# A denser routing product, a new order in the token blocks and a longer tile pipeline in a mixture-of-experts kernel

## The chip, the cores and the metric

One core of one Trainium2 chip runs the kernel. The metric is the device time of one execution in microseconds, lower is better. TensorE is called PE, VectorE DVE, ScalarE ACT, GpSimd POOL and SyncE SP. All of them run their own queue of instructions in order and meet at semaphores.

## The reference

```python
def reference(...):                       # x is (2, 2048, 256) f32
    x = x + attention(layernorm(x))       # 16 heads, causal; the change does not touch it
    xf = layernorm(x).reshape(-1, 256)    # 4096 tokens
    for j in range(2):
        residual = xf
        gate = xf @ router_W[j] + router_b[j]                  # 6 experts
        _, ids = top_k(gate + gate_bias[j], 2)
        sel = (ids[:, :, None] == arange(6)).any(axis=1)
        weights = softmax(where(sel, gate, -inf))
        h = einsum('nh,ehi->eni', xf, exp_Wup) + exp_bup[:, None, :]
        h = silu(einsum('eni,eij->enj', h, exp_Wg) + exp_bg[:, None, :]) * h
        eo = einsum('eni,eih->enh', h, exp_Wdown) + exp_bdown[:, None, :]
        s = (xf @ share_Wup + share_bup).reshape(-1, 2, 256)   # the shared expert
        s = silu(s @ share_Wg + share_bg) * s
        share_out = (s @ share_Wdown + share_bdown).sum(axis=1)
        y = residual + einsum('ne,enh->nh', weights, eo) + share_out
        xf = y * rsqrt(mean(y * y) + 1e-6) * norm_w[j]
    return x + xf.reshape(x.shape)
```

## The kernel before

`build_attention` comes first and leaves its result in DRAM (y_latent). `build_tokens`, the mixture, does the rest, and every edit is in it. It has two rounds c, one for each pass of the reference's loop. A round has eight blocks r of 512 tokens (blocks 0 to 7, then 8 to 15) and then 69 tiles t of 128 rows. A number in float32 is split into a high and a low part in the type fp32r (`_hi` by ACT, `_lo` by DVE or POOL as a difference), and a product is the sum of high x high, high x low and low x high.

A block of tokens. `turn(r)` turns the normalized tokens on PE into PSUM banks 6 and 7, `xt_hi` and `xt_lo` copy them to `xt`. `route(r)` (L1631) multiplies them with the router's weights; `choose(r)` (from L2258 to L2279) ranks six experts per token on DVE, `tanh` on ACT and `weigh` on DVE make the two weights. `shared_up(r, k)` for k = 0 to 3 (L1666) makes two products of 6 matmuls each with 512 columns; `silu(r, k)` (L1887) on ACT and `gated(r, k)` (L2403) on DVE take them up and free their banks, so that `shared_up(k)` waits for `gated(k - 2)`. `add_gated`, `g_hi` (L1901), `g_lo` (L2085, POOL) and `shared_down(r - 1)` (L1691), one block later, complete the shared expert, and `take_shared` adds it. In the first round `project(r + 2)` (L1595) multiplies attention's output for a block two ahead, `residual`, `moments` and `layernorm` (L2237) prepare it, and `make_experts` (r < 3) multiplies weights. `turn(r + 1)` waits for `layernorm(r + 1)`.

In blocks 9 to 12 DVE also adds the experts' rows to the token rows of the first round, four units of 128 tokens a block (`add_first` L2484, `add_second` L2492), ACT squares them (`square`, L2004), `variance` (L2499), `rms` (POOL) and `normalize` (L2508) end a block of the first round. POOL fetches those rows (`gather`, L2105) in blocks 8 to 11. After half of a round's blocks PE counts tokens per expert (`count`, L1701 and L1702), DVE numbers places (`take_counts`, `total_before`, `first_tiles`, `places`, `slots`, `tile_experts`), and POOL scatters the token rows into the order of the experts (`scatter`, L2092, 32 transfers for each half round), half of them in the blocks and half in the tile loop.

A tile. SP loads 128 rows into one of four buffers: `load_tile(t + 3)`, then `store_tile(t - 3)` in each round of its loop. It reads:

```python
for t in range(first, first + TILES):
    if t + 3 < first + TILES:
        load_tile(t + 3)
    if t >= first + 3:
        store_tile(t - 3)      # waits until ACT's tile_out(t - 3) is done
```

PE, in each round t: `tile_up(t)` (L1789), `tile_down(t - 2)` (L1780, L1819), `turn_gated(t - 1)` (L1802), `turn_tile(t + 2)` (L1775). ACT: `tile_silu(t)` (L1968), `tile_ghi(t - 1)` (L1974), `tile_hi(t + 2)` (L1962), `tile_seed(t + 2)` (L1989), `tile_out(t - 2)` (L1996). DVE: `tile_gated(t)` (L2585), `tile_glo(t - 1)` (L2589), `tile_lo(t + 2)` (L2578). Every eighth round PE and ACT read the next eight experts' numbers (`load_experts`). In the second half of a loop the units of the other half round and large transfers of kept rows are worked in (`UNITS_AT`, `ACC_AT`, `STORE_AT`). The last tiles' results are used after the loop. Blocks 14 and 15 (`LATE`) do only their routing in the blocks, and their shared expert after the second tile loop.

Of the kernel before, what the change touches and what calls it, by code (L numbers as in the profile page):

```python
# [27 lines left out]
P = 128  # L28
# [4 lines left out]
ROUNDS = 2  # L33
# [1250 lines left out]
def build_tokens(nc, W, F, w, x_v, out_v, y_v, last_sums, x_slots, e_slots, acc_dram, x1_dram, bias_dram):  # L1284

    with ExitStack() as ctx:
# [7 lines left out]
                 "routed", "logits", "route", "diff", "tanh",  # L1294
# [55 lines left out]
        small_total = DMA * (len(small) + ROUNDS)  # L1350

# [30 lines left out]
        with nc.Block() as block:  # L1382
# [201 lines left out]
            def _(pe):  # L1584
# [37 lines left out]
                def route(r):  # L1622
# [4 lines left out]
                    pe.wait_ge(S["xt_lo"], 2 * r + 2)  # L1627
                    for j in range(TPB):
                        terms = [(x, b, dt) for x, b in ((0, 0), (0, 1), (1, 0)) for dt in range(DT)]
                        for n, (x, b, dt) in enumerate(terms):  # L1630
                            mm = pe.matmul(ps[:, T_BANK, j * 8:j * 8 + E], xt[:, x, dt, j * P:(j + 1) * P],  # L1631
                                           W["router"][:, b, c, dt, :], start=n == 0, stop=n == len(terms) - 1)
                    mm.then_inc(S["routed"], 1)

                def shared_up(r, ks):
                    for k in ks:
# [8 lines left out]
                        if k == 1 and r and r % QB == 0:  # L1645
                            pe.wait_ge(S["counted"], r // QB)
# [49 lines left out]
                def count(g):  # L1696

                    pe.wait_ge(S["gated"], 4 * min(QB * g + QB, LATE[0]))
                    pe.wait_ge(S["route"], ROUTE_STEPS * (QB * g + QB - 1) + 9)
                    mask = F["chosen"][:, g % 2].rearrange("p j e -> p (j e)")  # L1700
                    pe.matmul(ps[:, COUNT_BANK, 0:JT * E], W["before"][:, :], mask, start=True, stop=True)  # L1701
                    pe.matmul(ps[:, COUNT_BANK, JT * E:2 * JT * E], W["count"][:, 1:2].broadcast_to([P, P]), mask, start=True, stop=True).then_inc(S["counts"], 1)  # L1702
# [38 lines left out]
                def block_of(r):  # L1741
                    route(r)
                    if r not in LATE:
                        shared_up(r, range(3))
                    if r == LATE[0]:
                        shared_down(r - 1)
                    if (r + 1) % 8:
# [9 lines left out]
                    if r % QB == QB - 1:  # L1757
# [4 lines left out]
                def turn_tile(t):  # L1762
# [7 lines left out]
                    if s == 0:  # L1770
                        pe.wait_ge(S["counted"], 2 * c + 2)
# [33 lines left out]
                def tile_down(t):  # L1805
# [6 lines left out]
                    else:  # L1812
                        pe.wait_ge(S["logits"], 8 * (t // TILES + 1))
                        pe.wait_ge(S["xt_lo"], 16 * (t // TILES + 1))
# [1020 lines left out]
```

## Time and profile before

| | |
|---|---|
| median of 3 timed runs | 2691.86 us (2691.54 to 2694.76) |
| the profiled execution's own time | 2688.85 us |
| its span, first to last instruction | 2687.1 us |
| busy: PE, PEld, POOL, DVE, ACT | 94%, 78%, 70%, 72%, 66% |
| mean granted TensorE clock | 0.966 |
| instructions | 44362 |

PEld is the load of weights into TensorE, which overlaps PE. Attention ends near 1734 us of the span. The granted clock is given as a share of 2.4 GHz; 0.5 is the lower of its two levels, 1.2 GHz. Times in the rows are counted in us from the start of the span.

### The profile page before, as it was taken

Reading aid. Unit: us, or ns where it says so; the run is one execution under the profiler, and the core shown is the slowest. Engines: PE = TensorE matmul, PEld = TensorE weight load, DVE = VectorE, ACT = ScalarE, POOL = GpSimd, SP = SyncE. Lnnn points to the kernel's source line nnn. Section 1 sums busy time; section 2 is a strip of 40 time slices with the busy share of each in tenths; the row PEclk is TensorE's granted clock in tenths of the full one; section 3 lists DMA queues with packets and bytes.
Section 4 is the critical chain, followed back from the end, with each engine's and each line's share of the span. In section 5 each row is a group of like instructions: output and inputs, shape, how many; then the busy total and the mean of one; then the engine's idle time right before and its main releaser. Section 6 shows DMA issues by size and latency. Waiting matters only on the chain. (4 is left out here: it accounts for less than half of the span.)

```text
span 2687.1 us, 44362 instructions
## 1 busy us (share of the span) xinstructions
PE 2523.9 (94%) x12650; PEld 2108.8 (78%) x12650; DVE 1944.3 (72%) x4167; ACT 1772.0 (66%) x3858; POOL 1867.9 (70%) x1612
## 2 busy tenths in 40 slices
PE   5999999999999999999999999899998998889985
PEld 4888888888777788888888888688887877778874
DVE  7888888888877788888888888355765454755466
ACT  3888888888768788888788888632325663226662
POOL 3989989889879798898898898722363142554135
PEclk8999999999999999999999999899999998879997
DMA  3112112112111111111111111254354461225543
GB/s 80 34 43 45 43 39 48 37 26 52 38 37 34 26 27 28 26 31 33 25 33 29 21 25 25 60 174 143 98 167 136 137 186 46 71 100 179 169 150 122
DMA packets 168047, 189.63 MB, mean 71 GB/s; under 512 B 57523, under 2 KB 140345, under 8 KB 167302
## 3 DMA queue, kind: packets, MB, share of 16 engines
q1 hardware_dynamic: 154502, 152.96, 20.8%
q0 software_dynamic: 12288, 33.57, 3.9%
q8 instruction: 113, 1.85, 0.3%
q14 instruction: 120, 0.98, 0.1%
q10 hardware_dynamic: 1024, 0.26, 0.0%
HBM read 114.06 MB, written 81.17 MB: 73 GB/s over the span
## 5 line engine op out<-in xcount | busy, mean ns | idle before, releaser
L382 POOL TENSOR_TENSOR pl<-pr,ph 128x512 fp32r<-128x512 f32 (+1 forms) x1024 | 1300.7, 1293 | 182.5 <-ACT ph L860 165.2
L857 ACT ACTIVATE pr<-ps 128x512 f32<-128x512 f32 (+1 forms) x1152 | 664.1, 577 | 290.1 <-DVE ps L1046 145.9
L1133 DVE TENSOR_REDUCE part<-ps 128x1 f32<-128x512 f32 (+2 forms) x1152 | 697.4, 618 | 83.3 <-PE ps L571 67.4
L860 ACT ACTIVATE ph<-ps 128x512 fp32r<-128x512 f32 (+1 forms) x1152 | 664.8, 577 | 0.0
L571 PE MATMUL ps<-k_hi,q_parts 128*128 128x512 f32 (+3 forms) x1280 | 472.9, 370 | 27.2 <-DVE part L1133 10.5
L585 PE MATMUL ps<-q_row,k_lo 65*128 65x512 f32 (+1 forms) x1152 | 443.7, 385 | 0.0
L584 PE MATMUL ps<-q_parts,k_hi 128*128 128x512 f32 (+1 forms) x1152 | 442.9, 384 | 0.0
L571 PEld LDWEIGHTS ps<-k_hi,q_parts 128*128 128x128 f32 x1280 | 242.7, 190 | 92.2 <-DVE part L1133 19.7
L584 PEld LDWEIGHTS ps<-q_parts,k_hi 128*128 128x128 f32 x1152 | 217.4, 189 | 42.5
L585 PEld LDWEIGHTS ps<-q_row,k_lo 65*128 65x128 f32 x1152 | 217.2, 189 | 25.4
L1789 PE MATMUL ps<-exp_up,yy 128*128 x828 | 232.7, 417 | 2.4 <-ACT yy L1962 2.0
L601 PE MATMUL ps<-ph,nn 128*128 128x512 f32 x576 | 226.0, 392 | 1.9 <-POOL pl L382 1.5
L1666 PE MATMUL ps<-xt,share_up 128*128 128x512 f32 x720 | 206.8, 449 | 21.0 <-DVE work L2403 19.8
L601 PE MATMUL ps<-ph,v_hi 128*128 128x512 f32 x576 | 223.9, 389 | 0.8 <-POOL pl L382 0.8
L2105 POOL DMA_INDIRECT yg<-e_slots,slot_i x96 | 94.8, 987 | 185.9 <-DMA e_slots<-work 128.9
L603 PE MATMUL ps<-pl,nn 128*128 128x512 f32 x576 | 219.7, 381 | 0.0
L603 PE MATMUL ps<-pl,v_hi 128*128 128x512 f32 x576 | 219.6, 381 | 0.0
L602 PE MATMUL ps<-ph,nn 128*128 128x512 f32 x576 | 218.6, 379 | 0.0
L602 PE MATMUL ps<-ph,v_lo 128*128 128x512 f32 x576 | 218.2, 379 | 0.0
L1130 DVE TENSOR_TENSOR ps<-ps,mask_rows 128x128 f32<-128x128 f32 x512 | 149.3, 292 | 84.5 <-PE ps L571 81.5
L1666 PEld LDWEIGHTS ps<-xt,share_up 128*128 128x128 f32 x720 | 154.1, 219 | 62.1 <-DVE work L2403 23.3
L956 POOL TENSOR_TENSOR q_parts<-q_raw,q_parts 64x512 fp32r<-64x512 f32 x128 | 174.3, 1362 | 28.2 <-DVE q_parts L1039 18.3
(279 smaller groups left out, 4426.4 us busy)
## 6 DMA issues: line engine op xcount, KB each, us to landing
work<-x_slots SPq DMA_DIRECT2D x138, 128.0 KB
e_slots<-work SPq DMA_DIRECT2D x138, 128.0 KB, 1.7
y_latent<-y_sums SPq DMA_DIRECT2D x128, 128.0 KB, 2.4
yg<-y_latent SPq DMA_DIRECT2D x32, 512.0 KB, 5.2
rec<-recip_rows SPq DMA_DIRECT2D x127, 128.0 KB, 3.1
x_slots<-zero_rows SPq DMA_DIRECT2D x32, 276.0 KB, 3.8
acc_shared<-accw SPq DMA_DIRECT2D x14, 512.0 KB, 3.1
xcur<-acc_shared SPq DMA_DIRECT2D x12, 512.0 KB, 3.8
```

Source lines behind the costliest of these rows:

```text
L382: eng.tensor_tensor(pl[:, s % RING, 0:w], pr[:, s % PR_RING, 0:w], f32(ph[:, s % RING, 0:w]), ALU.subtract).then_inc(sem, 1)
L571: pe.matmul(ps[:, max_bank(n), 0:w], qa[:, b, head, j * P:(j + 1) * P], khs[seq][:, at:at + w], start=True, stop=True).then_inc(S["max_sco ...
L584: pe.matmul(out, khs[p // PAIRS][:, k], qa[:, b, :, off:QW], start=True, stop=False)
L585: pe.matmul(out, kls[p // PAIRS][0:LD + 1, k], qc[:, b, :, off:QW], start=False, stop=True).then_inc(S["scored"], 1)
L601: pe.matmul(out, v_hi[:, kt, :], hi, start=kt == 0, stop=False)
L602: pe.matmul(out, v_lo[:, kt, :], hi, start=False, stop=False)
L603: pe.matmul(out, v_hi[:, kt, :], lo, start=False, stop=kt == 2 * b + 1).then_inc(S["latent_used"], 1)
L857: act.activation(pr[:, s % PR_RING, 0:w], src, ACT.Exp).then_inc(S["probs"], 1)
L860: act.activation(ph[:, s % RING, 0:w], src, ACT.Exp).then_inc(S["probs_hi"], 1)
L1133: dve.tensor_reduce(dst, src[:, 0:w], AX.X, ALU.max).then_inc(S["max_read"], 1)
L1666: mm = pe.matmul(out, sup[:, a, kind, n, dt, m * P:(m + 1) * P], x_t[:, x, dt, :], start=i == 0, stop=i == len(terms) - 1)
L1789: mm = pe.matmul(out, tx[:, t % 2, x, dt, :], wu[:, b, bass.ds(expert[t], 1), dt, :], start=False, stop=n == len(terms) - 1, skip_group_ch ...
```

## The change

- The router's high and low parts stand side by side (12 columns for a pass and half of the depth). `route` takes 128 columns from there as the stationary operand (what follows the 12 is not used) and moves 512 tokens: 4 matmuls of 512 columns that fill bank 6 with logits as rows. ACT's new `logits_back` copies the bank to `logits_t`, PE's new `turn_logits` turns it back in four transposes into bank 7, behind `shared_up(r, 0)`. `choose` adds high and low parts, one more operation.
- Orders in a block. ACT: `logits_back` first, `tanh` behind `silu(1)`, `xt_hi` ahead of `silu(3)`. DVE: `gated(0)` ahead of `choose`, `gated(1)` ahead of `weigh`, two of four units earlier, `normalize` behind `gated(2)`, `xt_lo` ahead of `gated(3)`. POOL: gathers ahead of `g_lo`, spread over blocks 8 to 12 by `GATHERS`.
- Tiles: `turn_gated`, `tile_ghi` and `tile_glo` take tile t - 2 in place of t - 1, `tile_down` and `tile_out` tile t - 3 in place of t - 2; `UNITS_AT` is one later. SP's loop is as it was.
- The count of a round's second half moves from the end of block 7 or 15 into the loop of tiles, behind `tile_up(first)`, in bank 7.

```diff
+        logits_t = accr[:, 1, 2:4, :].rearrange("p j d -> p (j d)")
...
+        def count_bank(g):
+            return T_BANK + 1 if g % 2 else COUNT_BANK
...
+                    terms = [(x, dt) for x in range(2) for dt in range(DT)]
+                    for n, (x, dt) in enumerate(terms):
+                        mm = pe.matmul(ps[:, T_BANK, :], W["router_wide"][c][dt], xt[:, x, dt, :], start=n == 0, stop=n == len(terms) - 1)
+                    mm.then_inc(S["routed_t"], 1)
+
+                def turn_logits(r):
+                    pe.wait_ge(S["logits_t"], r + 1)
                     for j in range(TPB):
-                        terms = [(x, b, dt) for x, b in ((0, 0), (0, 1), (1, 0)) for dt in range(DT)]
-                        for n, (x, b, dt) in enumerate(terms):
-                            mm = pe.matmul(ps[:, T_BANK, j * 8:j * 8 + E], xt[:, x, dt, j * P:(j + 1) * P],
-                                           W["router"][:, b, c, dt, :], start=n == 0, stop=n == len(terms) - 1)
+                        mm = pe.transpose(ps[:, T_BANK + 1, j * P:(j + 1) * P], logits_t[:, j * P:(j + 1) * P], ident[:, :])
                     mm.then_inc(S["routed"], 1)
...
                 def block_of(r):                      # PE
                     route(r)
                     if r not in LATE:
-                        shared_up(r, range(3))
+                        shared_up(r, range(1))
                     if r == LATE[0]:
                         shared_down(r - 1)
+                    turn_logits(r)
+                    if r not in LATE:
+                        shared_up(r, range(1, 3))
...
-                    if s == 0:
-                        pe.wait_ge(S["counted"], 2 * c + 2)
...
-                    for t in range(first, end + 2):   # PE's tiles
+                    for t in range(first, end + 3):
                         if t < end:
                             tile_up(t)
                         if t == 0:
                             shared_down(7)
-                        if t - 2 >= first:
-                            tile_down(t - 2)
-                        if first <= t - 1 < end:
-                            turn_gated(t - 1)
+                        if t == first:
+                            count(2 * c + 1)
+                        if t - 3 >= first:
+                            tile_down(t - 3)
+                        if first <= t - 2 < end:
+                            turn_gated(t - 2)
                         if t + 2 < end:
                             turn_tile(t + 2)
...
+                def logits_back(r):                   # ACT
+                    act.wait_ge(S["routed_t"], r + 1)
+                    if r:
+                        act.wait_ge(S["routed"], r)
+                    act.activation(logits_t, ps[:, T_BANK, :], ACT.Copy).then_inc(S["logits_t"], 1)
...
                 def block_of(r):                      # ACT
+                    logits_back(r)
                     if r + 2 < 8:
                         for pair in range(4):
                             split_y(r + 2, pair)
                     if r not in LATE:
                         silu(r, 0)
+                        silu(r, 1)
                     tanh(r)
                     if r not in LATE:
-                        for k in range(1, 4):
-                            silu(r, k)
+                        silu(r, 2)
                     if (r + 1) % 8:
                         xt_hi(r + 1)
                     if r not in LATE:
+                        silu(r, 3)
                         g_hi(r)
...
                 def block_of(r):                      # DVE
+                    if r not in LATE:
+                        gated(r, 0)
                     choose(r)
                     if r not in LATE:
-                        gated(r, 0)
+                        gated(r, 1)
                     weigh(r)
-                    if r not in LATE:
-                        gated(r, 1)
                     if r + 1 < 8:
                         layernorm(r + 1)
-                    if 10 <= r < 14:
-                        normalize(r - 6)
+                    if 9 <= r < 12:
+                        units(r, 0, 2)
...
                     if r not in LATE:
                         gated(r, 2)
-                        gated(r, 3)
+                    if 10 <= r < 14:
+                        normalize(r - 6)
                     if (r + 1) % 8:
                         xt_lo(r + 1)
+                    if r not in LATE:
+                        gated(r, 3)
...
+GATHERS = {8: range(16, 20), 9: range(20, 22), 10: range(22, 26), 11: range(26, 30), 12: range(30, 32)}
-UNITS_AT = [FIRST_DONE + 4 + 13 * u // 8 for u in range(JT)]
+UNITS_AT = [FIRST_DONE + 5 + 13 * u // 8 for u in range(JT)]
```

## Rows read from the trace of the kernel before

**Rows 1.** Stretches: length, busy time by engine (instructions), clock, DMA share, GB/s.
```profile
1775.43:2025.00 249.57, 240.45 (x1458) 209.33 (x1456) 154.61 (x379) 75.37 (x133) 92.86 (x77) 0.94 0.42 137
2025.00:2242.80 217.80, 198.33 (x1205) 172.60 (x1206) 115.14 (x298) 136.06 (x384) 70.12 (x70) 0.98 0.47 146
2242.80:2410.10 167.30, 141.94 (x689) 120.88 (x689) 101.88 (x267) 40.24 (x91) 83.64 (x80) 0.81 0.21 71
2410.10:2622.00 211.90, 194.67 (x1170) 168.10 (x1171) 111.42 (x297) 132.24 (x375) 67.31 (x68) 0.98 0.51 161
2622.00:2687.10 65.10, 34.72 (x165) 29.24 (x164) 45.19 (x100) 17.78 (x49) 37.73 (x37) 0.76 0.40 125
```

**Rows 2.** Waits of PE, 2235 to 2408: us in total, times, longest.
```profile
PE ps L1666 <- DVE work L2403: 14.1, 4, 4.7
PE ps L1631 <- DVE xt L2244: 7.1, 3, 2.9
```

**Rows 3.** Chain that ended last, in block 3: start, us, what.
```profile
1884.62 2.77 PE ps L1631 x24
...
1898.33 2.80 PE ps L1666 x12
```

**Rows 4.** Stretches, as in rows 1: a routing product and what follows.
```profile
1980.60:1983.40 2.80, 2.80 (x27) 2.80 (x26) 2.50 (x6) 0.00 (x0) 2.19 (x3) 1.00 0.40 149
1983.40:1986.80 3.40, 3.40 (x9) 2.62 (x9) 3.05 (x19) 0.00 (x0) 2.88 (x4) 0.50 0.60 224
```

**Rows 5.** Timeline of PE in block 3: start, us, operation.
```profile
1884.55 2.84 PE L1631 MATMUL ps<-router,xt 128*128 128x6 f32 x24
...
1897.30 1.03 PE L1619 MATMUL ps<-ident,xcur 128*128 128x128 f32 x8
```

**Rows 6.** Timeline of DVE in block 3.
```profile
1889.02 0.17 DVE L2258 TENSOR_TENSOR gate<-ps,router_b 128x24 f32<-128x24 f32 x1
...
1896.08 1.37 DVE L2237 TENSOR_SCALAR xcur<-x_table,mv,rs 128x256 f32<-128x256 f32 x4
```

**Rows 7.** Stretches, as in rows 1, from `variance` to `variance`.
```profile
2294.88:2319.25 24.37, 20.63 (x99) 17.38 (x99) 16.56 (x38) 6.99 (x18) 11.66 (x12) 0.79 0.20 65
2319.25:2341.05 21.80, 19.63 (x104) 16.60 (x102) 16.46 (x38) 6.95 (x17) 11.62 (x12) 0.86 0.22 72
```

**Rows 8.** Timeline of POOL, the first scatter of the second block stage.
```profile
2355.21 1.05 POOL L2092 DMA_INDIRECT x_slots<-xcur,slot_i  x1 [6.03 <-DVE slot_i L2368]
```

**Rows 9.** Chain that ended last, at the second tile loop.
```profile
2405.58 2.40 DMA x_slots<-xcur,slot_i
...
2408.00 2.05 DMA work<-x_slots
```

**Rows 10.** Timeline of PE in a steady round of the first tile loop.
```profile
2146.30 1.64 PE L1789 MATMUL ps<-exp_up,yy 128*128 x6
...
2148.83 0.38 PE L1775 MATMUL ps<-ident,work 128*128 128x128 f32 x2
```

**Rows 11.** Timeline of SP in that round.
```profile
2150.87 0.43 SPq L1453 DMA_DIRECT2D work<-x_slots  x1
```

**Rows 12.** Chain that ended last, loads of a tile.
```profile
2037.58 2.93 DMA work<-x_slots
...
2159.54 5.31 DMA work<-x_slots
...
2471.32 7.17 DMA work<-x_slots
...
2595.42 4.34 DMA work<-x_slots
```

**Rows 13.** DMA issues, 2025 to 2235: count, KB each, median us to landing.
```profile
e_slots<-work SPq DMA_DIRECT2D x66, 128.0 KB, 1.7
xcur<-acc_shared SPq DMA_DIRECT2D x8, 512.0 KB, 3.8
```

**Rows 14.** Timeline of ACT in the first tile loop.
```profile
2157.77 0.60 ACT L1989 ACTIVATE ps<-x_table 128x512 f32 x1 [1.51 <-issue]
```

**Rows 15.** Timeline of PE at the end of that loop.
```profile
2235.72 0.35 PE L1780 MATMUL ps<-bias,pick 128*128 128x256 f32 x1 [0.98 <-ACT nn L1974]
```

More of the change, by code:

```diff
@@ L1696, in count @@
                 def count(g):
[L1698 to L1699 removed]
+                    if g % 2 == 0:
+                        pe.wait_ge(S["gated"], 4 * (QB * g + QB))
+                    pe.wait_ge(S["route"], ROUTE_STEPS * (QB * g + QB - 1) + 10)
                     mask = F["chosen"][:, g % 2].rearrange("p j e -> p (j e)")
[L1701 to L1702 removed]
+                    bank = count_bank(g)
+                    if g % 2:
+                        pe.wait_ge(S["logits"], QB * g + QB)
+                    pe.matmul(ps[:, bank, 0:JT * E], W["before"][:, :], mask, start=True, stop=True)
+                    pe.matmul(ps[:, bank, JT * E:2 * JT * E], W["count"][:, 1:2].broadcast_to([P, P]), mask, start=True, stop=True).then_inc(S["counts"], 1)
                 def make_shared():
@@ L2012, in tiles @@
                     tile_hi(first + 1)
-                    for t in range(first, end + 2):
+                    for t in range(first, end + 3):
                         if t < end:
                             tile_silu(t)
-                        if first <= t - 1 < end:
-                            tile_ghi(t - 1)
+                        if first <= t - 2 < end:
+                            tile_ghi(t - 2)
                         if t + 2 < end:
@@ L2020, in tiles @@
                             tile_seed(t + 2)
-                        if t - 2 >= first:
-                            tile_out(t - 2)
+                        if t - 3 >= first:
+                            tile_out(t - 3)
                         u = unit_at(t - first, c)
@@ L2122, in block_of @@
                         y_lo_odd(r + 2, 3)
+                    for u in GATHERS.get(r, ()):
+                        gather(u)
                     g, q = r // QB - 1, r % QB
@@ L2549, in block_of @@
                     if 9 <= r < 13:
-                        for u in range(16 + 4 * (r - 9), 20 + 4 * (r - 9)):
-                            add_first(u)
-                            add_second(u)
+                        units(r, 2 if r < 12 else 0, 4)
                         variance(r - 5)
@@ L2595, in tiles @@
                     tile_lo(first + 1)
-                    for t in range(first, end + 1):
+                    for t in range(first, end + 2):
                         if t < end:
@@ L2688, in _ @@
                 late_lo(15)
-                units((55,))
+                late_units((55,))
                 take_shared(14)
```

81 lines of the change are left out of this document (43 added, 38 removed).

## The prediction

> **What bounds the kernel now.** I read the table of stretches first, cut where the code changes from one stage to the next [rows 1]. The change touches nothing in attention, the first two thirds of the span. What follows are four stages and a tail: eight token blocks (1775 to 2025), 69 expert tiles (to 2243), eight blocks (to 2410), 69 tiles (to 2622), and the last two blocks' late part. PE is busy 96% of the first block stage, 91 and 92% of the tile loops, 85% of the second block stage, and its clock is lowest in the two of those that hold the sparse routing product. The list of what PE waited for in the second block stage then says what stops it there: `shared_up` waits 14.1 us for DVE's `gated`, `route` 7.1 us for `xt_lo` [rows 2]. So the blocks of the first stage are bound by PE with DVE close behind, those of the second by DVE, whose queue is in order, and the tile loops by PE with one tile per 2.66 us.
>
> **Routing product.** Before, 24 matmuls of six columns take 2.77 us a block; 12 matmuls of 512 columns take 2.80 [rows 3], 0.233 each. The new product is four of these, 0.93 us, and four transposes at about 0.1 each. That is 1.4 us less on PE a block. Beside it stands the clock. In the stretch of the 24 small products PE is 100% busy and has its full clock; right behind it the granted clock is 0.50 for 3.4 us, 1.2 in place of 2.4 GHz, and 3.4 us at half speed lose 1.7 [rows 4]. The engine was not idle; what differs from `shared_up` is that six columns were moved and not 512. I take it that the dense product takes this away. The Trainium skill (TensorE: Matmul & The Clock Gate, "Part 1: The HAM clock gate") says that activity releases the throttle and an idle stretch brings it back. Read as busy or idle that rule would not have slowed this stretch, and the dense product would give nothing of the 1.7 back; the stage's mean clock of 0.94 [rows 1] means some 30 us at half clock, of which I put a bit over half behind `route`, 8.5 us lost, and by that rule the sum below would come out as much higher. The trace does not agree with so coarse a reading.
>
> **First block stage.** PE does not get all of that, because the answer now makes a round trip. ACT copies the logits (some 0.6), PE turns them behind `shared_up(0)`, and DVE's `choose` can start 4.4 us after the block, and `gated(0)` now stands ahead of it. Take block 3. `turn` starts 12.75 us after `route` [rows 5]. PE alone would need 0.93 + 2.8 + 0.4 + 5.6 = 9.7. But `turn(r+1)` waits for `layernorm(r+1)`, which is behind `gated(0)`, `choose` and `gated(1)` on DVE. Before, `choose` to `layernorm` starts 7.06 us apart, and the latter takes 1.37 [rows 6]. After: `gated(0)` ends at 5.3, `choose` (4.6 with POOL's subtractions beside it, and one more operation of 0.2) at 10.1, `gated(1)` 0.7, `weigh` 0.2, `layernorm` 1.4, hence `turn` at about 11.9. The block gains 0.9, not 3. In block 1, which has twice the slow clock, it comes to some 3.8; in block 4, where DVE first numbers the tiles, 2.5 (a third of PE's 2.5 us wait stays); block 6 has no y to split, 2.4; block 7 next to nothing, as ACT's new copy is queued behind `split_down` and its weights' DMA, and PE then waits 5 us for the logits. Sum 0.6 + 3.8 + 1.1 + 0.9 + 2.5 + 0.5 + 2.4 + 0.4, less one slow stretch where PE waits, is **11 us**. Bounds: 4 (0.5 a block) and 25 (8 times 1.4 + 1.7).
>
> **Second block stage.** Blocks 8 and 9 lose the wait for `xt_lo`, now ahead of `gated(3)` on DVE as `xt_hi` is ahead of `silu(3)` on ACT: about 2.85 of each. They also lose the slow clock behind `route`. I make block 8 16.8 long where it took 22.6, and block 9 6.6 shorter up to its `variance`. From there the period goes from `variance` to `variance`: 24.37 us for block 10, 21.80 for 11, with DVE busy 16.6 and 16.5 [rows 7]. The new period is DVE's 16.6 and what it must wait for: the four squares on ACT, behind which `logits_back` is now queued, the copy and `silu(0)` (some 2.3 together), and 1 us for `shared_down` and for ACT's `g_hi` with its squares. That is 19.9: 4.5 and 1.9 less. PE waits for the logits instead of for `gated`, 3.6 us a block: the stall has moved, and only shrunk. Then slot numbers come 1.6 us earlier still. So the first scatter, at 2355.21 before [rows 8], comes 20.4 us earlier. From it the second tile loop hangs on POOL: the last scatter is issued at 2405.58, lands 2.40 later, and the tile's load takes 2.05 [rows 9]. These 50.4 us hold 32 issues at 1.27, two `g_lo` at 2.5, two `rms` at 1.05 and near 3 us of waiting, of which half can go. Together **22 us**; bounds 12 (a period of 22) and 32 (period of DVE's busy time). The moved gathers are 8 issues a block as before and fit into POOL's idle time.
>
> **Tile loops: turn at two, down at three.** PE does the same work per tile. No wait of `turn_gated` for `gated` stood in the loops' lists, so its later place gives nothing. `gated(t)` now waits until tile t-2 is turned, in the same round; that is 0.7 us later and ends before the seed needs it: nothing. But SP stores tile t-3 and then loads tile t+4, and the store waits for `tile_out`, which comes one round later. Before, in the steady loop, a load is issued at 2150.87, 4.57 us after the start of the round at 2146.30, and `turn_tile` stands 2.53 into a round [rows 10, 11]. Before, the tile loaded is turned three rounds on, 3 x 2.66 + 2.53 - 4.57 = 5.94 us after the issue; after the change two rounds on, **3.28 us**. Nothing else in SP's order is changed. Loads took 2.93, 5.31, 7.17 and 4.34 us where the chain shows them [rows 12]; quiet ones 2.05. So a quiet load still hides, a disturbed one does not. What disturbs them: the eight or so 512 KB transfers of each loop, which take 3.8 us against 1.7 for a store of a tile's size [rows 13] (a load right behind one takes by my estimate 3.3 and has 0.5 less lead: 0.5 us each, 8 us in both loops); ACT's reading of the experts' numbers, 1.51 us in every eighth round [rows 14], which leaves such loads a lead near 2.1 (0.3 each, 5 in all); and the three long ones of the chain, each one tile nearer (2.8 + 2.7 + 2.7 = 8). That makes **+21 us**; bounds 0 (all loads quiet) and 45 (every second tile of both loops' last 40 late by 4.34 - 3.28). A stall moves only the next tile's need, so it can come again two tiles on. The Trainium skill (DMA: Bandwidth & Descriptors, "Anatomy of one DMA") gives a DMA a fixed cost of about 2.0 us and 436 GB/s: by that 128 KB take 2.3, an estimate, under the new lead. The quiet loads agree, the four of the chain do not.
>
> **Ends of the loops, and the rest.** With no `tile_up` between, each of the last tiles waits 0.98 us for `ghi` and `glo` [rows 15]. There were two such waits, now three, and one tile more to multiply down (1.05), which the loop's start saves: +1.3 a loop, **+2.6**. Stalls over some 2.5 us will bring the half clock back now and then: **+3**. `count` inside the loop costs its 0.4 us there instead of before it; units and stores one tile later stay hidden in the loop; dearer router copies (48 columns) are at the start and under DMA. The tail is unchanged: 0.
>
> **Sum.** -11 - 22 + 21 + 2.6 + 3 = -6.4 us. The profiled execution took 2688.85 (span 2687.1 and 1.75 around it); its successor would take 2682.5. The median of the runs is 3.0 above the profiled one, so for timed runs I forecast 2685.5, said as **2686**.
>
> **Rivals.**
> *The loads are in time.* Then the loops pay only the 5 us of the number reads. For it: the loads with nothing beside them land in 2.05. Against it: four of the chain's. Time 2686 - 16 = 2670.
> *The shorter lead decides (slower).* SP's load is late in every second tile while gathers run, and each stall is worth 1.06: 40 us in place of 21, with 2 more of slow clock. Time 2686 + 21 = 2707. It turns the sign from 27 us of stalls on. For it: a mean DMA share of 0.47 and 0.51 in the loops [rows 1], where a load meets other transfers as often as not; against: a stall gives the DMAs time.
> *The copy of the logits costs what the product saves.* PE waits at `turn_logits` in each block from 10 on (behind the squares), in block 7 and wherever `split_y` waits for DMA; the blocks' gain of 33 is halved. Time 2686 + 16 = 2702. For it: ACT is in order, and squares come last in the old queue; against: the wait it replaces was of like length.
>
> **Numbers.** What a measurement of this kernel can tell is some 0.2%, 5.4 us. Forecast as worked out 0.42, loads in time 0.20, lead decides 0.22, copy costs the gain 0.16. The forecast's own range is 2677 to 2695. All cases but the outermost fifth lie in 2663 to 2710. Of the forecast's 0.42, 0.26 lie under 2686.5, 0.14 within 0.2%, 0.02 above; of the third case 0.03 and of the fourth 0.04 lie within. With the loads in time that is faster 0.46, same 0.21, slower 0.33.
>
> **What would show it.** Right: no half clock right behind `route` in the stage 1775 to 2025; `turn` some 11.9 us after `route` in block 3; `variance` to `variance` near 19.9; PE's list naming ACT's logits copy; the first scatter of the second block stage 92 us behind its start, where it was 112; and in the loops `turn_tile` waiting for the x_slots loads, the loops 10 to 14 us longer each. Wrong: loops of the old length (loads hidden), or blocks of the old length.

## The result, and the profile after

Timed together, the kernel before takes 2691.70 us (median, 2689.39 to 2694.76) and the changed one 2708.41 us (2705.62 to 2712.74), four executions each: a ratio of 1.0064, 95% interval [1.0046, 1.0082]. It is slower by 16.7 us, three times what a measurement can tell, where the forecast was 6 us faster. The profiled execution of the changed kernel was the slowest of its four (2712.74, span 2711.0), and that of before among the fastest, so the two traces lie 23.9 us apart: they say where the time went, and some 7 us of it is scatter between executions.

The stretches of the changed kernel, cut at the same places of the code (the columns are those of [rows 1]):

```profile
1777.00:2021.36 244.36, 223.53 (x1327) 189.16 (x1326) 153.15 (x388) 82.54 (x147) 95.02 (x79) 0.97 0.43 142
2021.36:2259.87 238.51, 209.08 (x1209) 179.12 (x1210) 111.86 (x296) 138.04 (x379) 69.18 (x71) 0.94 0.42 131
2259.87:2411.11 151.24, 116.09 (x556) 95.03 (x557) 101.26 (x274) 44.05 (x99) 81.69 (x79) 0.88 0.23 78
2411.11:2645.00 233.89, 201.94 (x1175) 171.00 (x1176) 109.64 (x298) 135.50 (x375) 66.73 (x68) 0.96 0.46 146
2645.00:2711.00 66.00, 32.59 (x165) 27.27 (x163) 45.09 (x100) 17.78 (x49) 39.45 (x37) 0.79 0.40 124
```

The first tile's transposes come 2.36 us behind the cut of [rows 1] in the trace of before. Cut there, its first tile loop is:

```profile
2027.36:2242.80 215.44, 198.33 (x1205) 172.59 (x1206) 113.72 (x295) 133.70 (x379) 67.92 (x69) 0.98 0.46 145
```

So the first block stage went from 251.9 us (1775.43 to 2027.36) to 244.4, the first tile loop from 215.4 to 238.5, the second block stage from 167.3 to 151.2, the second loop from 211.9 to 233.9 and the tail from 65.1 to 66.0: -7.6, +23.1, -16.1, +22.0, +0.9, and 1.6 in attention, which the change does not touch. The blocks gave less than was forecast (23.7 us in both stages, where 33 were), and the loops took more by 45.1, where 26.6 were forecast. In the loops PE's busy time rose by 18.0 us (393.0 to 411.0) for the same tiles, and its idle time by 27.0.

What PE waited for in the two loops, before and then after (from just behind the first tile; us in total, times, longest):

```profile
PE ps L1775 <- DMA work<-x_slots: 3.3, 2, 2.3
...
PE ps L1775 <- DMA work<-x_slots: 4.2, 2, 3.0
```

```profile
PE ps L1790 <- DMA work<-x_slots: 16.9, 13, 2.4
...
PE ps L1790 <- DMA work<-x_slots: 18.6, 14, 5.2
```

Four waits for a tile's load have become 27, and 7.5 us 35.5. Of the 27, 14 are for a load that SP issued right behind a large transfer of kept rows, seven in each loop: 11.4 us in the first (of its eight transfers of 512 KB) and 9.5 in the second. Where they come from, the chain that ended last shows at 2164 us (start, us, what; SPq is SP's queue of DMA issues):

```profile
2164.05 0.32 SPq L1463
...
2164.41 0.43 SPq L1471
...
2164.89 5.55 DMA work<-x_slots
...
2170.58 0.41 PE ps L1790 x2
```

SP stores a tile (L1463), issues a 512 KB load of kept rows (L1471), and only then the next tile's load, which takes 5.55 us; PE turns the tile 0.14 us after it lands. Two neighbouring stretches show what the wait costs besides itself:

```profile
2168.00:2171.60 3.60, 1.41 (x9) 1.04 (x8) 0.93 (x3) 1.39 (x6) 0.95 (x1) 1.00 0.71 253
2171.60:2175.00 3.40, 3.40 (x14) 3.07 (x13) 1.14 (x3) 1.48 (x5) 1.32 (x2) 0.50 0.27 80
```

In the first PE has its full clock and is idle 2.2 us; in the second it is busy throughout at a granted clock of 0.50, and the six matmuls of `tile_up` take 2.27 us in place of 1.65.

In the second block stage the list of PE's waits, to be held against [rows 2], is now:

```profile
PE ps L1642 <- ACT accr L1911: 17.5, 5, 7.4
PE ps L1635 <- DVE xt L2268: 8.8, 4, 3.9
PE ps L1701 <- POOL gg L2110: 4.0, 1, 4.0
```

The wait for `gated` (14.1 us) is all but gone (1.3 us) and a wait for ACT's copy of the logits stands there. From `variance` to `variance` (columns as in [rows 7]):

```profile
2302.11:2324.48 22.37, 19.04 (x88) 15.77 (x88) 16.77 (x40) 7.37 (x19) 11.52 (x11) 0.86 0.22 71
2324.48:2346.16 21.68, 18.81 (x92) 15.52 (x92) 16.78 (x40) 7.37 (x19) 11.55 (x11) 0.92 0.23 74
```

Block 3 of the first stage, against [rows 5]; and the stretch right behind a routing product, against [rows 4]:

```profile
1881.48 1.19 PE L1635 MATMUL ps<-xt,share_down_router 128*128 128x512 f32 x4
...
1893.34 1.32 PE L1624 MATMUL ps<-ident,xcur 128*128 128x128 f32 x8 [1.82 <-DVE xcur L2261]
```

```profile
1882.50:1886.00 3.50, 3.50 (x19) 2.84 (x18) 2.95 (x12) 2.74 (x6) 0.00 (x0) 1.00 0.02 5
```

`turn` starts 11.9 us behind `route`, as forecast, and no half clock follows the product.

### The profile page after: what moved, and what is told of

It is laid out like the page before. It is cut to its first block and busy times, and to the rows that moved or that the text cites. A ratio compares the mean times of both kernels' runs of the same rounds, so it can differ in the third digit from the quotient of the medians.

```text
span 2711.0 us, 43895 instructions
## 1 busy us (share of the span) xinstructions
PE 2500.4 (92%) x12394; PEld 2073.8 (76%) x12394; DVE 1938.4 (72%) x4183; ACT 1788.3 (66%) x3874; POOL 1869.2 (69%) x1612
## 3 DMA queue, kind: packets, MB, share of 16 engines
q1 hardware_dynamic: 154502, 152.96, 20.7%
## 5 line engine op out<-in xcount | busy, mean ns | idle before, releaser
L1130 DVE TENSOR_TENSOR ps<-ps,mask_rows 128x128 f32<-128x128 f32 x512 | 149.4, 292 | 84.5 <-PE ps L571 81.8
L956 POOL TENSOR_TENSOR q_parts<-q_raw,q_parts 64x512 fp32r<-64x512 f32 x128 | 174.5, 1363 | 28.6 <-DVE q_parts L1039 18.6
L1676 PE MATMUL ps<-xt,share_up 128*128 128x512 f32 x720 | 188.1, 416 | 5.7 <-DVE x_table L2241 1.9
L2617 DVE TENSOR_TENSOR work<-ps,work 128x256 f32<-128x256 f32 x138 | 58.5, 424 | 188.5 <-PE ps L1817 144.9
```

What stands on the lines that cost most here:

```text
L1676: mm = pe.matmul(out, sup[:, a, kind, n, dt, m * P:(m + 1) * P], x_t[:, x, dt, :], start=i == 0, stop=i == len(terms) - 1)
```

## The experiments

Unless said otherwise a diff is against the changed kernel. Ratios are to the kernel before, run beside it; the changed kernel's own is 1.0064 [1.0046, 1.0082].

### The lead of the loads and the depth of the pipeline

**e1_lead_back**: SP's stores one tile later.

```diff
-                        if t >= first + 3:
-                            store_tile(t - 3)
+                        if t >= first + 4:
+                            store_tile(t - 4)
```

> The changed kernel with SP's stores one tile later (store of tile t-4 behind the load of tile t+3, where it was t-3), so that a tile's load is issued about 5.9 us ahead of its transposes again, as before the change; turning at two behind and multiplying down at three behind stay. Theory A, the shorter lead costs what the loops lost: PE's wait for the x_slots loads (21.1 us in the first loop, 23.5 in the second) falls to under 5 us a loop, the loops take about 220 and 215 us instead of 238.5 and 233.9, and the time is 2708 - 38 = about 2670 us. Theory B, the three-deep pipeline itself costs it (its waits between gated, ghi, glo and down): the loops keep over 230 us and the time stays within 5 us of 2708. Theory C, the loads are late because the transfers around them are slow, whatever the lead: a few us back, 2700.

**e2_lead_cut**: the kernel before, with `store_tile(t - 2)` there in place of `store_tile(t - 3)`.

> The kernel before with SP's stores one tile earlier (store of tile t-2 behind the load of tile t+3, where it was t-3): nothing else is changed, so the load of a tile is issued about 3.3 us ahead of its transposes where it was 5.9. Theory A, the shorter lead alone makes the loss of the tile loops: PE waits some 20 us in each loop for the x_slots loads and the time is 2692 + 40 = about 2732 us (2722 to 2742). Theory B, the three-deep pipeline makes it: within 5 us of 2692. Between them by the forecast on record (21 us for the lead): 2713.

**e3_tiles_only**: the kernel before with PE's, ACT's and DVE's loops of the change (`tile_down(t - 3)`, `turn_gated(t - 2)` and their partners).

> The kernel before with the tile loops of the changed one alone (turning at two, multiplying down at three behind, units one tile later); the routing product, the order in the blocks and the place of the count stay as before. If the two parts of the change add up, this is 2692 + 45 (the loops' loss in the two traces, drains included) = about 2735 us, and the waits for x_slots loads are near 20 us a loop. By the terms on record (+21, +2.6, +3) it would be 2719. If the loops lose only together with the blocks' part (earlier scatters, the count inside), it stays near 2695.

**e4_blocks_only**: the changed kernel with those loops as before.

> The changed kernel with the tile loops of the kernel before (turning at one, multiplying down at two behind, units as before); routing product, orders in the blocks and the later count stay changed. By the stretches of the two traces the blocks gained 7.6 + 16.0 = 23.6 us: about 2668 us. By the terms on record (-11 and -22) 2659. If the count inside the loop, or the blocks' new orders, had any part in the loops' loss, it is over 2675.

| kernel | median | ratio |
|---|---|---|
| e1_lead_back | 2675.37 | 0.9929 [0.9902, 0.9956] |
| e2_lead_cut | 2720.91 | 1.0106 [1.0074, 1.0138] |
| e3_tiles_only | 2730.18 | 1.0136 [1.0109, 1.0162] |
| e4_blocks_only | 2669.21 | 0.991 [0.9885, 0.9935] |

All four ran on one chip, where before took 2693.76. The two parts of the change pull apart: +36.4 us for the tile part (e3) and -24.6 for the rest (e4), together +11.9 where both at once gave +16.7. Theory A holds: with the old lead (e1) the changed kernel is 33 us faster by the medians, which come from two chips, and 36 by the ratios, and the old pipeline with the short lead (e2) is 27 us slower than the kernel before. Theory B is left with a small share. With the lead short the deeper pipeline costs 9.3 us more (e3 against e2), with the lead long 6.2 (e1 against e4); the intervals of each pair overlap, so that neither is resolved by itself, but both have the same sign.

In e1 PE's waits for loads fall to 2.8 and 4.5 us, and both loops shrink to near the 220 and 215 us of Theory A:

```profile
2022.03:2240.78 218.75, 200.91 (x1210) 173.93 (x1210) 110.87 (x296) 136.64 (x379) 68.70 (x71) 0.96 0.46 143
2391.77:2610.30 218.53, 197.84 (x1174) 169.61 (x1175) 108.73 (x298) 134.45 (x375) 66.81 (x68) 0.97 0.50 157
```

The stretches of both loops of e2 and then of e4:

```profile
2031.83:2265.23 233.40, 207.32 (x1205) 178.32 (x1206) 114.82 (x295) 135.21 (x379) 67.92 (x69) 0.94 0.42 134
2427.72:2654.00 226.28, 199.56 (x1172) 169.98 (x1173) 112.51 (x297) 133.79 (x375) 67.46 (x68) 0.97 0.48 151
```

```profile
2022.96:2237.97 215.01, 198.85 (x1209) 172.46 (x1210) 114.37 (x296) 134.01 (x379) 69.00 (x70) 0.98 0.46 145
2387.41:2602.30 214.89, 197.31 (x1176) 169.94 (x1177) 111.95 (x298) 132.85 (x376) 67.21 (x68) 0.97 0.51 159
```

The shorter lead alone brings PE's busy time from 393.0 to 406.9 us and the clock of the first loop from 0.98 to 0.94. With the long lead it is 396.2 in e4 and 398.8 in e1, which keeps the deeper pipeline. Most of the longer PE time of the changed loops (411.0) follows the stalls, then, and is not work that the change added.

### Which loads are late

The lead was the cause, but which loads were late at it was open.

**i1_acc_quarter** (on the changed kernel) and **i2_before_quarter** (on the kernel before):

```diff
-                    sp.dma_start(acc_rows(r), acc_dram[r]).then_inc(S[f"acc_in{r % 8}"], DMA)
+                    part = slice(0, 1) if r < 8 else slice(0, TPB)
+                    sp.dma_start(acc_rows(r)[:, part, :], acc_dram[r][:, part, :]).then_inc(S[f"acc_in{r % 8}"], DMA)
```

Both kernels leave three quarters of those rows unloaded, so their results are not the program's.

> The changed kernel with the eight 512 KB transfers of kept rows in the first tile loop cut to a quarter (128 KB each); the other three quarters of those rows are not loaded, so that part of the first round's result comes from stale rows. Theory A, a tile's load right behind such a transfer is what is late at the shorter lead: in the trace of the change such loads took 4.8 to 5.6 us against a lead of 3.3, some 2 us each where the forecast had 0.5, and half clock follows; about 16 to 20 us less than the changed kernel run beside it, all between 2133 and 2230 us. Theory B, gathers and scatters delay the loads and the 512 KB only happen to stand there: 4 us less or nothing.

> The same cut of the eight transfers in the kernel before, as a control. Theory A: with 5.9 us of lead the loads behind them hide, as they took no more than 5.3 us there: 1 to 4 us less than before, for the waits that its list names (3.3 us in that loop). If it gains as much as i1 gains on the changed kernel, the transfers cost the same at either lead and Theory A falls.

**i3_acc_ahead**: the large loads ahead of the store in SP's round, all bytes kept.

```diff
-                        if t >= first + 3:
-                            store_tile(t - 3)
                         i = t - first
                         if c == 0 and i in ACC_AT:
                             load_acc(ACC_AT[i])
...
                             load_x1(X1_AT[i])
+                        if t >= first + 3:
+                            store_tile(t - 3)
```

> The changed kernel with each 512 KB load of kept rows issued ahead of the store of tile t-3 in SP's round, where it was behind it: right behind the load of tile t+3, so that the next tile's load, which waits for that store, no longer follows it at once. Lead and pipeline depth stay. Theory A: the large transfer is mostly over when the next load starts, 10 to 20 us of the 17 to 20 that the change lost come back. Theory B, its data collide with the load before it just as well: within 4 us of the changed kernel.

**i4_after_again**: the changed kernel once more, on the chip of the i kernels.

> The changed kernel again, on the same chip as i1 and i3, to compare them with: 1.0064 of before.

| kernel | median | ratio |
|---|---|---|
| i4_after_again | 2712.58 | 1.0071 [1.0051, 1.0091] |
| i1_acc_quarter | 2702.81 | 1.0045 [1.0029, 1.0062] |
| i3_acc_ahead | 2693.63 | 1.0008 [0.9998, 1.0017] |
| i2_before_quarter | 2690.15 | 0.9993 [0.9981, 1.0005] |

Cutting the transfers gives 9.8 us back in the changed kernel by the medians (7 by the ratios, whose intervals overlap), less than the 16 to 20 of Theory A, and 2.0 in the kernel before (2692.13 on this chip), which its interval does not tell from nothing: the long lead hides them, the short one does not. Moving them out of the way of the next load gives 19 us back, nearly all of the 20.5 that the changed kernel loses on this chip, with the lead and the depth unchanged; i3 moves the large loads of both loops, i1 cuts those of the first alone. The first tile loop of i4, then of i1, then of i3, with the second loop of i3 behind it:

```profile
2024.46:2262.77 238.31, 207.73 (x1210) 177.73 (x1210) 111.99 (x296) 137.74 (x379) 68.75 (x71) 0.94 0.42 131
```

```profile
2021.09:2245.98 224.89, 202.07 (x1210) 173.29 (x1210) 111.81 (x296) 137.44 (x379) 67.71 (x70) 0.98 0.40 125
```

```profile
2019.97:2244.95 224.98, 201.99 (x1209) 173.18 (x1210) 111.46 (x296) 137.49 (x379) 69.83 (x71) 0.97 0.44 139
2394.68:2623.00 228.32, 201.76 (x1177) 170.91 (x1177) 109.98 (x301) 136.12 (x378) 66.83 (x68) 0.97 0.48 150
```

In the traces i1 and i3 make the first loop 13.4 and 13.3 us shorter, i3 the second some 6. So of the 23 us that the first loop lost, 13 hang on eight loads that stand right behind a 512 KB transfer: 1.7 us each by the traces, 1.2 by i1's medians, against 0.5 in the forecast. PE's busy time has 5.7 of these 13 (207.7 to 202.1 and 202.0), so that the 1.7 holds 0.7 that is not waiting. Of the remaining 10 some 3 are there with the long lead too (218.8 us in e1, 215.4 before). In i3 PE still waits 9.9 us for loads, in ten waits; whether the gathers and scatters make those, as Theory B has it, no run shows.

The eight 512 KB transfers are all in i3's loop, and it is as short as i1's: what counted was what SP had issued just ahead of the tile's load. The Trainium skill (DMA: Bandwidth & Descriptors, "Queues, rings and completion order") says that SP owns one row of rings, one on each DMA engine, and that each engine consumes a ring's descriptors in order. The times of i3 fit that; no trace here shows the rings themselves.

### What the blocks' parts are worth

All but g4 stand on e4_blocks_only.

**g3_product_only**: the orders of ACT, DVE and POOL in the blocks as before, the dense product and the later count kept.

> As e4_blocks_only, but the orders in the blocks as before on ACT, DVE and POOL (the dense product with its copy and its transposes stays, as does the later count). By the reasons on record the product gives 1.4 us a block on PE and the slow clock behind it, 8 to 10 us in the first stage if nothing else waits; but the logits now come later to a DVE that starts a block with choose. Theory A, the product carries most of the first stage's gain: 0.995 of before, 2679 us. Theory B, with the old orders the round trip of the logits costs what the product saves: 0.999 to 1.001, and the gain of 24 us needs both parts.

**g4_order_only**: the kernel before, with the new orders alone. It ran beside g3, g1 and g2, on another chip than e4.

> The kernel before with the new orders in the blocks on ACT, DVE and POOL alone: the sparse routing product, the place of the count and the tile loops are as before. Slow clock behind route stays (0.94 in the first block stage). Theory A, the orders make most of the second stage's gain (PE's waits for xt_lo and gated) and nothing in the first: 12 us, 0.9955 of before, 2680 us. Theory B, they are of use only with the dense product, whose late logits they cover: within 3 us of before.

g3: 2700.68 us, 1.0041 [1.0027, 1.0054]. g4: 2671.06 us, 0.9929 [0.9915, 0.9942]. Neither theory on g3 went far enough: the dense product, with the later count, makes the kernel 11.5 us slower. On g4 Theory A has the direction, with half again its size, 18.1 us. On top of the orders the product is worth 5 us by the ratios (0.991 against 0.9929), and the intervals overlap. Both block stages of g3, of g4, and of e4, which has both:

```profile
1777.98:2040.43 262.45, 229.02 (x1326) 194.24 (x1325) 157.89 (x388) 82.18 (x147) 95.77 (x79) 0.94 0.41 133
2255.93:2421.69 165.76, 124.58 (x556) 101.14 (x556) 102.01 (x271) 43.70 (x97) 83.30 (x80) 0.83 0.21 72
```

```profile
1780.78:2031.94 251.16, 239.72 (x1458) 206.28 (x1457) 148.71 (x381) 77.76 (x137) 94.52 (x79) 0.95 0.41 136
2248.82:2397.90 149.08, 133.02 (x688) 114.95 (x688) 102.36 (x267) 40.36 (x91) 83.99 (x79) 0.84 0.24 80
```

```profile
1778.51:2022.96 244.45, 222.88 (x1326) 188.82 (x1324) 152.90 (x388) 82.54 (x147) 95.84 (x79) 0.98 0.43 143
2237.97:2387.41 149.44, 116.59 (x556) 95.84 (x557) 101.34 (x274) 43.44 (x98) 82.34 (x79) 0.88 0.24 80
```

In the first stage the product alone takes 10.5 us more than before, as DVE starts with `choose` and waits for the logits: PE's list there has 20.4 us of waiting for `gated`, and the stage's clock stays at 0.94 though no sparse product is left. The orders alone give 0.8 and both 7.5. In the second stage the orders give everything (167.3 to 149.1) and the product nothing (149.4), though it takes 16.4 us off PE's busy time (133.0 to 116.6). As the blocks stand in e4, PE's work did not set that stage; g1 shows what did.

**g1_logits_first**: `logits_back(r + 1)` ahead of the four squares of block r on ACT, and so for blocks 10 to 13 no longer at their own start. Shown against e4_blocks_only:

```diff
                     if 9 <= r < 13:
+                        logits_back(r + 1)
                         for u in range(16 + 4 * (r - 9), 20 + 4 * (r - 9)):
                             square(u)
```

> The changed kernel with the old tile loops (as e4_blocks_only, 0.991 of before, 2669 us), and ACT's copy of the logits of blocks 10 to 13 ahead of the four squares that stood before it in the queue; PE waited 16.8 us in four waits for this copy. Theory A, this wait of PE's sets the pace of the second block stage: the wait goes and 12 to 16 us come back, 2655 us, 0.986 of before. Theory B, DVE's queue sets it and PE waits because it has nothing to do: DVE's gated(1) loses its wait of about 1.1 us a block and no more, 3 to 4 us come back, 2665 us, 0.9895.

**h3_logits_again**: the same kernel, beside the h kernels.

> The kernel of g1_logits_first once more, to stand beside h1_both and h2_lead_longer on one chip. 0.988 of before, 2657 us; a second value shows how far ratios of different chips differ.

g1: 2657.54 us, 0.9881 [0.9866, 0.9896]; h3: 2659.42 us, 0.9882 [0.9867, 0.9898]. 7.8 us come back by the ratios, between the theories. ACT's copy in block 10 was issued behind the last square, which waited for DVE's last unit (e4, then g1):

```profile
2277.64 0.42 ACT L2029 ACTIVATE junk<-xcur 128x256 f32<-128x256 f32 x1 [1.41 <-DVE xcur L2518]
2277.97 0.19 ACT L2029 ACTIVATION_READ_ACCUMULATOR junk<-xcur 128x1 f32 x1
2278.06 0.58 ACT L1911 ACTIVATE accr<-ps 128x512 f32<-128x512 f32 x1
```

```profile
2273.97 0.58 ACT L1911 ACTIVATE accr<-ps 128x512 f32<-128x512 f32 x1
```

In this block the copy comes 3.6 us sooner behind `route` (6.57 to 2.93), and the stage is 9.0 us shorter:

```profile
2237.23:2377.68 140.45, 113.95 (x557) 92.45 (x557) 100.76 (x274) 43.17 (x98) 83.93 (x79) 0.90 0.25 85
```

PE's waits for the copy had been 16.8 us, so half of that was on the path; 7.4 us of waits for `gated` stand there now.

This changes what the product is worth. g4 and g1 ran on one chip: with the orders alone the time is 2671.06 us and the second stage 149.1, with the product and its copy ahead of the squares 2657.54 and 140.5. The product, with the later count, gives 13.5 us on top of the orders, 0.9881 [0.9866, 0.9896] against 0.9929 [0.9915, 0.9942], of which the second stage has 8.6 in the traces. In the changed kernel the place of one copy in ACT's queue took that away.

**g2_down_later**: `split_down` of the first three matrices behind `tanh` and `weigh` of block 7 on ACT and DVE.

> As e4_blocks_only, but ACT and DVE split the first three down matrices behind tanh and weigh of block 7, no longer at the end of block 6, where ACT waited for their transfers and PE then 4.6 us for the logits behind them. Theory A, that wait is lost time on the path: block 7 is 4 to 4.6 us shorter and the time about 2665 us, 0.9895 of before. Theory B, the end of the stage hangs on these transfers and not on block 7: the wait moves to silu(7, 2) or to the first tile and the time stays within 1 us of e4_blocks_only.

**h1_both**: g1 and g2 together.

> The changes of g1_logits_first and g2_down_later together, with the old tile loops. If both add up (7.8 us for the logits copy ahead of the squares; block 7 was 3.8 us shorter in the trace of g2, though its ratio to before came out as that of e4_blocks_only): 2654 us, 0.9868 of before, and 3 to 4 us under the kernel of g1 run beside it. If the later split of the down matrices only moves the wait: within 1 us of it.

g2: 2665.38 us, 0.9909 [0.9894, 0.9924]; by the ratio nothing, e4 has 0.991. Its median is that of Theory A, its ratio that of Theory B, and e4 ran on another chip. h1: 2653.67 us, 0.9864 [0.9843, 0.9884], 5.8 us under h3 on the same chip. The traces agree on block 7, from `route(7)` to the first tile, in h3 and then in h1:

```profile
1993.73:2019.34 25.61, 17.29 (x83) 14.11 (x81) 13.99 (x33) 9.18 (x17) 10.83 (x10) 0.92 0.62 207
```

```profile
1997.36:2019.73 22.37, 15.60 (x83) 12.99 (x81) 15.57 (x34) 9.52 (x17) 11.47 (x10) 0.97 0.72 241
```

The 3.2 us there are what Theory A of g2 said of block 7. The intervals of h1 and h3 overlap, so the timed gain is likely, not settled.

**h4_norm_first**: h1 with `layernorm(r + 1)` ahead of `choose(r)` on DVE.

> h1_both with DVE's layernorm of the next block ahead of choose in the first block stage; PE waited 8.3 us in six waits for it in turn. Theory A, DVE's chain gated(0), choose, gated(1), layernorm sets those blocks, as the prediction had it: turn comes 3 us earlier in blocks 3 and 4, and 4 to 8 us come back against h1_both. Theory B, choose and gated(1) come 1.4 us later and PE waits for gated instead, ahead of shared_up(2) and (3): within 2 us, or slower.

2657.77 us, 0.9876 [0.9861, 0.9891]: 4 us over h1, with intervals that overlap, and in the traces the first stage is 242.2 us against 241.6. What PE waited for in blocks 0 to 7 changed its name and kept its size (h1, then h4):

```profile
PE ps L1624 <- DVE xcur L2265: 8.0, 6, 3.4
```

```profile
PE ps L1676 <- DVE work L2433: 8.3, 7, 2.4
```

`turn` comes 2 us sooner in block 3 (9.9 behind `route`, 11.9 in h1), and nothing is gained. That is Theory B: where PE waits for DVE, an exchange inside DVE's queue chose only which wait is named.

### A version that beats both

**h2_lead_longer**: h1 with e1's edit to SP on the old loops, so that the lead is a round longer than it ever was.

> h1_both with SP's stores one tile later, two behind on PE: a load is issued about 8.6 us ahead of its transposes, where before the change it was 5.9. Theory A, what costs in the loops is a lead under the time of the slowest loads (4.3 to 7.2 us in the chain of before): 3 to 5 us less than h1_both, the loads' waits left in the loops (0.7 and 4.5 us) go. Theory B, at 5.9 the lead was long enough and the four long ones are bound by something else: within 1 us of h1_both.

2649.03 us (2645.19 to 2649.58), 0.9839 [0.9826, 0.9853], 4.6 us under h1. Behind the first tile PE's waits for loads in the second loop were 4.2 us in h1 and are 0.2 here, so Theory A is what the trace shows; the timed intervals of the two overlap. This is the fastest kernel of the study: 42 us under the kernel before and 59 under the changed one.

## Why the prediction was wrong

**Routing product and its clock: right.** `turn` at 11.9 us behind `route` in block 3, the half clock behind the product gone, the stage's clock up (0.94 to 0.97, and 0.98 in e4). [rows 4] foretold this: the engine had been busy all through the 24 small matmuls, and the half clock came behind them all the same. By the rule that the prediction takes from the Trainium skill (TensorE: Matmul & The Clock Gate, "Part 1: The HAM clock gate"), read as busy or idle, the new product would have changed nothing here; these stretches do not bear that reading out. The 11.9 us is in part luck. The prediction's own pieces (`choose` done at 10.1, then 0.7, 0.2 and 1.4) end at 12.4 and not at 11.9. In the trace `gated(0)` ends 6.1 us behind `route`, where 5.3 was forecast, and `turn` starts 0.55 us after `layernorm` does and not at its end.

**First block stage: -11 forecast, -7.6 measured.** From `route` to `route` the blocks gained 1.4, 3.0, 0.4, 0.6, -0.3, 0.2, 1.8 and 0.6. Block 4 is the largest miss (2.5 forecast): the wait of 2.5 us for `gated` in it became one of 3.4 for `layernorm`. h4 shows that removing one such wait need not shorten the stage.

**Second block stage: -22 forecast, -16 measured.** The period was to be 19.9 and is 22.4 and 21.7; the first scatter comes 98.7 us behind the stage's start, where 92 was forecast and 112.4 was before. The mechanism was named right (the copy is queued behind the squares, PE waits for it), and g1 prices it at 7.8 us, about what was missing. The product, and the slow clock that it takes away, counted for nothing in this stage as long as its copy stood behind the squares; the 8.6 us between g4 and g1 is what it could give.

**Tile loops: the step that failed.** The forecast put +21 for the shorter lead, +2.6 for the drains and +3 for more slow clock, 26.6 in all. The traces show 45.1; the change against e4 is 39 in timed runs. The mechanism was right to the instruction: the lead falls, and `turn_tile` waits for the x_slots loads. Two terms of the sum were too small.

The first is the +21 for the lead. PE's waits for loads rose by 28.0 us. The prediction had "a load right behind one takes by my estimate 3.3" and so "0.5 us each". It was an estimate where the trace had rows: the 5.31 us load of [rows 12] at 2159.54 is such a load, as SP's own queue at that time shows (L1466 is the 512 KB load):

```profile
2158.70 0.32 SPq L1458 DMA_DIRECT2D e_slots<-work  x1
2159.06 0.43 SPq L1466 DMA_DIRECT2D xcur<-acc_shared  x1
2159.54 0.45 SPq L1453 DMA_DIRECT2D work<-x_slots  x1
```

In the first loop of the change such loads took 3.71, 3.45, 3.61, 5.26, 5.55 and 4.79 in its chain. The seven that PE waited for cost 1.6 us of waiting each.

The second is the +3 for the slow clock. PE's busy time rose by 18.0 us. The text had stalls "over some 2.5 us" bring the half clock back "now and then"; the wait shown above is 2.2 long. The clock's own records in the traces give the size: in the two loops the clock was 0.50 for 20.7 us before and for 50.1 in the change, and PE was busy for 18.6 and 39.6 us of that. At full clock the 21.0 more would have taken half, so 10.5 us are the slow clock's, an estimate. In e1, with the long lead, PE was busy for 24.7 us at half clock, and in i1 the first loop's mean clock is back at 0.98: it follows the stalls. The two terms share their cause, and the 1.7 us that i1 and i3 put on a load behind a large transfer holds some of both. Where the changed loop had its full clock, from 2046.02 to 2104.99, PE was busy 54.8 us for 20 tiles and 54.2 before; that would be 4 of the other 7.5 us. The rest stays open.

**The sign.** With gains of 24 to 25 us (e4), the loops decide. At the forecast 26.6 us the time would have been about that of before; at 39 to 45 it is what was measured. The rival "the shorter lead decides (slower)" named this, at 2707 us, with a chance of 0.22. That its number lies within 2 us of the measured 2708.4 is luck, as two errors in it cancel. It had 40 us of stalls, one late load in two at 1.06 each, and 5 of slow clock; the run has 28.0 us more of waits, with 27 late loads of 138 at 1.3 each, and 18.0 more of PE's busy time. The rival on the copy of the logits had a real mechanism as well (g1), but it is not what turned the sign. "The loads are in time" is out. The fixed cost that the prediction takes from the Trainium skill (DMA: Bandwidth & Descriptors, "Anatomy of one DMA") is given there for DMAs that GpSimd issues, and these loads are SP's. The 2.3 us estimated from it fits the quiet loads (2.1 at the least, 2.4 in the median of the first loop) and not those right behind a large transfer (3.45 to 5.55).

## What to carry to other kernels

A pipeline made one stage deeper moves the last consumer's completion back, and whatever SP does behind it moves too: count how far ahead of its use each load is issued afterwards, and compare that with the slowest loads in the trace, those behind large transfers in the same queue first. If the lead shrinks, move the store or the large transfer out of the way of the load: the first gave 33 us back here (e1) and the second 19 (i3), where the whole change had cost 17. A routing product that took 16 us off PE's second block stage gave nothing there while its copy was queued behind other work, 8.6 us once the copy came first (g1 against g4), and was a loss where its longer round trip met the old order. Such a change and the orders that cover it are one change, to be tried together and priced apart.

## What the runs showed of the hardware that was not expected

- The place of a transfer in SP's queue mattered as much as its size: eight 512 KB loads issued right behind a tile's load, and no longer right ahead of one, gave 13.3 us in the first loop, as much as taking three quarters of their bytes away (13.4).
- A wait of 2.2 us on a PE otherwise busy was followed by 3.4 us at a granted clock of 0.50. A wait of 1.80 ahead of 2136.76 was too (0.50 from 2137.5 to 2140.9); one of 1.96 ahead of 2182.38 was not, and the next `tile_up` there took its usual time.
- DVE's unit operations took longer where POOL ran `g_lo` beside them: 1.41 and 1.48 us against 0.48. In block 9 of e4, with POOL's two operations from 2273.99 on for 2.82 us:

```profile
2273.77 0.48 DVE L2510 SCALAR_TENSOR_TENSOR xcur<-yg,mix,xcur 128x256 f32<-128x256 f32 x1
2274.28 1.41 DVE L2518 SCALAR_TENSOR_TENSOR xcur<-yg,mix,xcur 128x256 f32<-128x256 f32 x1
2275.61 1.48 DVE L2510 SCALAR_TENSOR_TENSOR xcur<-yg,mix,xcur 128x256 f32<-128x256 f32 x1
2277.13 0.48 DVE L2518 SCALAR_TENSOR_TENSOR xcur<-yg,mix,xcur 128x256 f32<-128x256 f32 x1
```
